# Eight layers on one core: output bias added tile by tile, residual joins reordered, token ids as one 16-bit value, expert weights held behind the second gather

## The reference, cut to what matters

```
x = x + cross_attention_0(norm(x));  x = x + quantised_ffn(norm(x))
x = x + (cross attention with bias, ffn)(norm(x))
x = x + L1_ffn(norm(x))      # LN, self-attention over 1024 keys, + o @ w_o + b_o; LN; top-2 of 8 experts, relu
x = x + L2_attention(norm(x)) # one head, 77 keys, integer mask
x = x + L2_ffn(norm(x))      # every expert whose sigmoid(x @ Wg + bg) > 0.5, relu
x = x + L3_attention(norm(x))
x = x + L3_ffn(norm(x))      # the best expert of 8, gelu
# an expert: y = func(x @ W1[e] + b1[e]) @ W2[e] + b2[e], weighted and added to its tokens
```

## Time and profile before

| | |
|---|---|
| median of 3 runs | 2282.51 us (2282.28 to 2283.62) |
| the profiled execution | 2278.04 us, its span 2276.3 us |
| PE busy | 1962.3 us, 86% |
| DVE, ACT, POOL busy | 47%, 40%, 33% |
| moved by DMA | 151.26 MB, mean 66 GB/s |
| m1, m2, m3 begin at | 984.8, 1375.2, 2076.0 us |

### The profile page before, as it was taken

The page is one execution under the profiler, slowest core; times in us unless marked ns, Lnnn a source line. Parts: engine busy times, 40 slices in busy tenths (PEclk is TensorE's granted clock), DMA queues, the critical chain, the costliest instruction groups (busy, mean ns, idle before and its releaser), DMA issues. The chain is left out here.

```text
span 2276.3 us, 39023 instructions
## 1 busy us (share of the span) xinstructions
PE 1962.3 (86%) x12253; PEld 1425.4 (63%) x12254; DVE 1069.3 (47%) x2424; ACT 910.1 (40%) x1930; POOL 755.3 (33%) x790
## 2 busy tenths in 40 slices
PE   6699989744999999849999945999999998696898
PEld 5476656512233232338999844999999997364797
DVE  6875834635777777253332246222222222576221
ACT  2413642132777777613333321333333333264132
POOL 0134952405000000043444333334444343585243
PEclk9799999876999999969999976999999999798899
DMA  4004300123111111075222118422122221205611
GB/s 159 19 1 146 101 1 1 32 76 94 37 36 49 42 37 36 2 245 156 33 35 36 28 53 292 115 36 36 31 36 35 35 34 27 68 1 177 221 32 26
DMA packets 124399, 151.26 MB, mean 66 GB/s; under 512 B 27066, under 2 KB 104731, under 8 KB 124171
## 3 DMA queue, kind: packets, MB, share of 16 engines
q1 hardware_dynamic: 93533, 117.61, 15.9%
q0 software_dynamic: 24288, 31.81, 8.6%
q10 hardware_dynamic: 6480, 0.59, 0.3%
HBM read 114.35 MB, written 37.36 MB: 67 GB/s over the span
## 5 line engine op out<-in xcount | busy, mean ns | idle before, releaser
L1902 PE MATMUL banks<-m_rowsT,x_normT 128*128 128x128 f32 x4032 | 479.0, 278 | 11.9 <-issue 7.6
L1902 PEld LDWEIGHTS banks<-m_rowsT,x_normT 128*128 128x128 f32 x4032 | 468.5, 194 | 29.0 <-issue 11.5
L1911 PE MATMUL banks<-m_w,m_hT 128*128 x2016 | 461.3, 382 | 7.3 <-ACT m_hT L2145 5.6
L1911 PEld LDWEIGHTS banks<-m_w,m_hT 128*128 128x128 f32 x2016 | 375.6, 191 | 56.4 <-issue 8.4
L2155 ACT ACTIVATE m_y<-banks,m_weight 128x256 f32<-128x256 f32 x126 | 59.6, 473 | 636.7 <-PE banks L1914 526.6
L2585 ACT ACTIVATE sh_pT<-banks 128x1024 f32<-128x1024 f32 x256 | 250.7, 1024 | 26.1 <-PE banks L2544 26.0
L2145 ACT ACTIVATE m_hT<-banks,m_bias 128x128 f32<-128x128 f32 x848 | 229.7, 387 | 65.6 <-PE banks L1902 61.4
L1821 POOL DMA_INDIRECT scratch_acc<-m_y,m_row_ids x106 | 169.6, 1600 | 124.8 <-ACT m_y L2155 82.9
L2609 DVE TENSOR_REDUCE sh_mhalf<-banks 128x1 f32<-128x512 f32 x308 | 194.2, 683 | 35.5 <-PE banks L2493 35.5
L2079 DVE TENSOR_SCALAR x_normT<-m_w 128x2048 f32 x129 | 158.3, 1227 | 77.0 <-issue 69.8
L1807 POOL COPY m_row_ids<-m_ids 128x1 int32 x117 | 52.1, 445 | 337.0 <-DMA scratch_acc<-m_y,m_row_ids 215.2
(11 more groups left out here) (404 smaller groups left out, 2745.1 us busy)
## 6 DMA issues: line engine op xcount, KB each, us to landing
m_w<-L_W SPq DMA_DIRECT2D x32, 1024.0 KB, 13.4
m_w<-L1f_W SPq DMA_DIRECT2D x16, 1024.0 KB, 13.6
a_bt<-bias SPq DMA_DIRECT2D x16, 616.0 KB, 3.9
scratch_parts<-sp_part SPq DMA_DIRECT2D x48, 128.0 KB, 1.9
sh_ks<-scratch_parts SPq DMA_DIRECT2D x96, 64.0 KB, 2.2
scratch_rows<-x_norm SPq DMA_DIRECT2D x12, 512.0 KB, 9.3
sh_qs<-scratch_parts SPq DMA_DIRECT2D x90, 64.0 KB, 2.3
scratch_acc<-x_resid SPq DMA_DIRECT2D x2, 2048.0 KB, 13.5
```

Of the source, the lines that this page charges most:

```text
L1902: mm = pe.matmul(ps[:, H_BANK[u] + f // 4, f % 4 * P:(f % 4 + 1) * P], w1_tile[:, u, k, f * P:(f + 1) * P], rowsT[:, u, k, :], start=(k == ...
L1911: mm = pe.matmul(ps[:, Y_BANK[u], 0:D], hT[:, u, f, :], w2_sb[:, bass.ds(e, 1), f, :], start=(f == 0), stop=(f == FB - 1 and not biased))
```

## The change

- The bias b_o is added to `xn` by 16 instructions, one tile each, each behind the `m_split` of one more pair of heads.
- `token_projection` adds x for 12 tiles, with `rstd` of the three groups after tiles 6, 10 and 11. The last four tiles are joined at the start of m1's POOL stream in one instruction, and DVE waits for it (`joined`) before it overwrites these tiles.
- `plain_cross_attention` makes no `rstd`; m2 makes all four groups itself (`ready=0` in place of 2).
- A token's id is one number in 16-bit floats of the other format (`F16`), 128 * tile + lane - 2048: one product instead of two per slot, a table half as wide on PE, and one instruction instead of two to read it.
- SP waits for `rows_in[1]` (the gather of slot 1 has landed) after the table's stores; only then follow expert 1, the store of x, and experts 2 to 7.

```diff
@@ routed_layer, SP
                     for g in range(NCH):
                         sp.wait_ge(tile_normed, 4 * g + 4)
                         sp.dma_start(table[g * CH:(g + 1) * CH, 0:D].rearrange("(t p) d -> p t d", p=P), xn[:, 4 * g:4 * g + 4]).then_inc(stored, 16)
+                    sp.wait_ge(rows_in[1], 16)
+                if e == 1:
                     sp.dma_start(stream.rearrange("(t p) d -> p t d", p=P), x[:]).then_inc(x_stored, 16)
@@ routed_layer, POOL
+            if joins_last:
+                pool.tensor_tensor(x[:, NT - 4:NT], x[:, NT - 4:NT], xn[:, NT - 4:NT], ALU.add).then_inc(joined, 1)
             for g in range(ready, NCH):
@@ routed_layer, PE
-                    at = ps[:, TABLE_BANK, g * 2 * W:(g + 1) * 2 * W] if local else ps[:, TABLE_BANK, 0:2 * W]
-                    mm = pe.matmul(at, lane_hits[:, g % 2, :, t], id_parts[:, g, :, :, t],
+                    at = ps[:, TABLE_BANK, g * W:(g + 1) * W] if local else ps[:, TABLE_BANK, 0:W]
+                    mm = pe.matmul(at, lane_hits[:, g % 2, :, t], tokens_at[:, g, :, t],
@@ routed_layer, DVE
             for t in range(NT):
+                if joins_last and t == NT - 4:
+                    dve.wait_ge(joined, 1)
...
-            link(dve.tensor_tensor(id_parts[:, :, 0], tile_hits, back_b[:].unsqueeze(1).unsqueeze(1).broadcast_to([P, G, W, NT]), ALU.mult))
-            dve.tensor_scalar(id_parts[:, :, 1], tile_hits, lane[:], None, ALU.mult).then_inc(parts_done, 1)
+            dve.tensor_tensor(tokens_at, tile_hits, tokens[:].unsqueeze(1).unsqueeze(1).broadcast_to([P, G, W, NT]), ALU.mult).then_inc(parts_done, 1)
...
-            link(dve.tensor_scalar(high_at, high, float(P), float(TOK), ALU.mult, ALU.add))
-            dve.tensor_tensor(ids_at, high_at, low, ALU.add).then_inc(ids_done, 1)
+            dve.tensor_scalar(ids[:, 0:COLS], ps[:, TABLE_BANK, 0:COLS], float(TOK), None, ALU.add).then_inc(ids_done, 1)
@@ self_attention, POOL
-                pool.tensor_tensor(acc[:], acc[:], w["bo"][:].unsqueeze(1).broadcast_to([P, NT, D]), ALU.add).then_inc(bias_added, 1)
+                for t in range(NT):
+                    pool.wait_ge(m_split, t + 1)
+                    pool.tensor_tensor(acc[:, t, :], acc[:, t, :], w["bo"][:], ALU.add).then_inc(bias_added, 1)
@@ program
-            routed_layer(core, "m2", "threshold", x, ..., ready=2)
+            routed_layer(core, "m2", "threshold", x, ..., ready=0)
```

More of the change, by code:

```diff
@@ L255, in __init__ @@
         self.rank, self.lane, self.counting = (self.loads[n] for n in ("rank", "lane", "counting"))
[L256 to L258 removed]
+        self.ones, self.before, self.lanes = sb("ones", [P, P], BF16), sb("before_b", [P, P], BF16), sb("lanes", [P, P], F16)
+        self.tiles, self.marked_tiles = sb("tiles", [P, 2 * NT + EXPERTS], F16), sb("marked_tiles", [P, NT], F16)
+        self.tokens, self.earlier = sb("tokens", [P, NT], F16), sb("earlier", [P, EXPERTS, EXPERTS])
         self.pick, self.pad_id, self.unit = sb("pick", [65, P], BF16), sb("pad_id", [P, 1]), sb("unit", [P, 1])
@@ L287, in make @@
         pool.tensor_scalar(self.marked_tiles[:], self.counting[:, 0:NT], -float(EXPERTS * NT), None, ALU.add).then_inc(made, 1)
-        pool.tensor_scalar(self.back[:], self.counting[:, 0:NT], -float(NT), None, ALU.add).then_inc(made, 1)
+        pool.tensor_scalar(self.firsts[:], self.counting[:, 0:NT], float(P), -float(TOK), ALU.mult, ALU.add).then_inc(made, 1)
+        pool.wait_ge(made, 13)
+        pool.tensor_scalar(self.tokens[:], self.firsts[:], self.lane[:], None, ALU.add).then_inc(made, 1)
     def order_experts(self, dve, made):
@@ L1263, in plain_cross_attention @@
         shares = sb("shares", [P, 4, D])
-        stats, moments, rstd, half = core.stats, core.moments, core.rstd, core.half
+        stats, moments = core.stats, core.moments
         params.place_passing(ctx)
-        b2_split, share_sb, joined, stats_done, moments_done, eps_done, rstd_done = (
-            sem(x) for x in ("b2_split", "share", "joined", "stats", "moments", "eps", "rstd"))
+        b2_split, share_sb, joined, stats_done, moments_done = (sem(x) for x in ("b2_split", "share", "joined", "stats", "moments"))
         s_mm, chain, s_ready, exp_done, rs_done, pT_mm, pT_sb, y_mm, y_sb = (
@@ L1280, in _ @@
             params.split_output_bias(pool, b2_split)
[L1282 to L1287, removed]
             for g in range(NCH):
@@ L1663, in routed_layer @@
         wg_sb, bg_sb, wide_gate = params["wg"], params["bg"], sb("wide_gate", [P, KD, 32])
[L1664 removed]
+        rank, counting, earlier = route.rank, route.counting, route.earlier
         if affine:
@@ L2718, in _, with reciprocals @@
         def _(pool):
-            for g in range(NCH):
+            def reciprocals(g):
                 own = slice(4 * g, 4 * g + 4)
-                if g < NCH - 1:
-                    pool.wait_ge(moments_done, 4 * g + 4)
-                    pool.tensor_scalar(rstd[:, own], moments[:, own, 1], EPS, None, ALU.add).then_inc(eps_done, 1)
-                    pool.wait_ge(eps_done, g + 1)
-                    pool.tensor_tensor(rstd[:, own], rstd[:, own], half[:].broadcast_to([P, 4]), ALU.pow).then_inc(rstd_done, 1)
-                for t in range(4 * g, 4 * g + 4):
-                    pool.wait_ge(y_sb, t + 1)
-                    pool.tensor_tensor(core.x[:, t, :], core.x[:, t, :], acc[:, t, :], ALU.add).then_inc(joined, 1)
+                pool.wait_ge(moments_done, 4 * g + 4)
+                pool.tensor_scalar(rstd[:, own], moments[:, own, 1], EPS, None, ALU.add).then_inc(eps_done, 1)
+                pool.wait_ge(eps_done, g + 1)
+                pool.tensor_tensor(rstd[:, own], rstd[:, own], half[:].broadcast_to([P, 4]), ALU.pow).then_inc(rstd_done, 1)
+            for t in range(NT - 4):
+                pool.wait_ge(y_sb, t + 1)
+                pool.tensor_tensor(core.x[:, t, :], core.x[:, t, :], acc[:, t, :], ALU.add).then_inc(joined, 1)
+                if t in (6, 10):
+                    reciprocals(t // 4 - 1)
+            reciprocals(2)
 def program(nc, dram):
```

33 lines of the change are left out of this document (13 added, 20 removed).

## The result

The changed kernel takes 2314.59 us (median of 4 runs, 2314.18 to 2316.72); the kernel before, run beside it, 2282.40 (4 runs, 2278.84 to 2283.62). The ratio is 1.0146, 95% interval 1.0128 to 1.0163: 32 us slower, where 41 were forecast. The profiled execution after has a span of 2314.9 us.

The account below looks back on a forecast made before the run. PE was taken as busy for most of the span, so gains come only where it stands still. Terms -7.8 - 5.9 - 0.7 + 37.8 + 17.9 = +41.3 us on a 2282.5 us median gave 2324 us, range 2301 to 2335.

Parts of the forecast that it names:

- The hold: Routed layers: SP's wait for slot 1's gather makes PE's first W1 product later, +37.8 us over m1, m2 and m3.
- T: Landing of slot 1's gather in each routed layer, forecast at 1020.0 in m1, 1414.1 in m2, 2103.7 us in m3.
- first product: PE's first product with W1 in each routed layer, claimed 18.2 us after slot 1's gather lands: +11.7, +14.9, +11.2 us.
- The fast rival: SP not held by bytes under way, eight issues of 0.4 to 0.5 us each: 2275 us, chance 0.08.
- The load moved into the slots: Slot 4 of each routed layer: its gather meets the shifted 16 MB load and PE stalls 7.4 us; +17.9 us over all.
- The bias: Self-attention: bias added tile by tile, so DVE's L2619 falls from 7.94 to 0.18 us; -7.8 us.
- no idle of PE ahead of L2502: Self-attention: sign that PE no longer waits there once L2619's longest is near 0.18 us.
- The joins: End of the projection: twelve joins fit beside it and the stage ends with DVE; -5.9 us.
- L2's attention and m2: No rstd between the attention's joins, -2.7 us; m2 makes four groups, +2.3 of which +2.0 taken; together -0.7 us.
- I count 0: Start of m1: four tiles joined there cost POOL 2.7 us, claimed covered by DVE's and PE's work; 0 us.
- The ids: Routed layers: narrower id table brings ids or first gather earlier by 3.1 us in m1, 0.8 in m2, 3.8 in m3.
- The sum: Whole kernel: all terms together +41.3 us, added to the median of 2282.5 us: 2324 us, slower by 1.8%.

## Why the prediction was right

**The direction and the step that decides it.** The hold moved the first step of `experts_ready` and the store of x behind T, with 8 MB ahead of the step. Forecast: first product at +11.7, +14.9 and +11.2 us; measured +11.7, +14.8 and +9.1. In m3 T came 0.4 us sooner than I had it, the step 14.3 us after T in place of 15.2, and the product 2.2 us after the step in place of 3.0. The fast rival (SP isn't held by bytes) is excluded by issues of 7.57 and 7.29 us and, as an experiment, by the 5.5 to 6.1 us per layer that 2 MB are worth.

**The load moved into the slots.** Forecast 17.9 us over the three layers. In the run with the hold alone the stages grew by 52.1 us and the first products came 12.0, 13.8 and 10.1 later, which leaves 16.1. The stall was 5.7 to 6.5 us there in place of 7.4; against the kernel before it grew by 13.9 us over the three layers. The low clock behind it, which my sum did not have, adds 3.0 (W2's products took 4.89, 4.97 and 5.32 us there, and 3.72, 3.72 and 4.76 at the same places before). So the total is partly luck: a stall that I had too long and a clock that I had left out nearly cancel. In the changed kernel the same subtraction leaves 19.3.

**The bias.** Forecast -7.8; alone it measured -8.3 in the medians (interval -10.3 to -3.2) and -9.8 in the stage. The traces bear out the 7.8 itself: PE's idle time fell from 8.59 to 0.82 us. My sign "no idle of PE ahead of L2502" was too strict. The further 2 us of the stage are not placed.

**The joins.** The end of the stage came nearly as forecast: -4.9 between the traces with the bias alone and the changed kernel (-5.9). So did L2's attention and m2: from POOL's first join to the start of m2 it took 12.4 us and now 9.6 (forecast -2.7), and DVE's last normalised tile in m2 comes 1.7 us later after its start (forecast +2.3, of which I took 2.0). The step that failed is "I count 0" for the four tiles in m1. I had judged by the mean pace of L1969 that it isn't locked out. By the Trainium skill's "SBUF — State Buffer", section "Who interferes with whom", a `tensor_scalar` can be, for the whole of a GpSimd instruction. The trace agrees with the page: 2454 ns in place of 401. The price was 2.0 us of DVE, and without the hold 3.5 of m1's first product (the joins alone), as the store of the gate weights starts 2.0 us later into a full queue and lands 4.2 later. With the hold the queue is empty and that part falls away; the 2.0 us of DVE do not, and there the earlier ids pay for them. Semaphores and barriers are thus not the only places where DVE and POOL meet.

**The ids.** Forecast -3.1, -0.8 and -3.8. The first two came in DVE's time (m1's 32 products take 2.75 us, L2047 is gone). Alone they measured nothing: in m1 and m3 the first gather waits for the store of the gate weights. I had written that of m3 and not asked it of m1, where the earlier trace rows don't show the wait ahead of the first gather. In the changed kernel they do count. SP's queue is empty, that store lands 3.0 us after its issue in m1 (13.6 before), and POOL's wait ahead of the first gather ends with the ids (7.49 us of it in the rows of m1 above, and the same releaser in m2 and m3). In m1 their 3.1 us are set against the 2.0 of the join's lock, so that T came only 0.4 us sooner than with the hold alone. In m3 the -3.8 came true (first gather at 23.0 in place of 26.8), but 3.3 of it come with the hold alone, which keeps SP's queue empty.

**The size.** The sum was +41.3, the stages of the two traces show +40.2, and the medians +32. The parts measured alone give +50.5 - 8.3 - 5.3 - 0.2 = +36.7 by medians; from t0 on their traces show +51.3, -5.6, -5.9 and +2.9, together +42.7. So the parts add up in the traces, and what the medians lack is 4 to 9 us. Of the 9, the two profiled executions account for 6.5 by their distance from their medians, 4.4 under and 2.1 over. What the hold costs within the changed kernel shows how such a gap comes about: 42.7 by medians and 42.0 between the two profiled executions, but 48.8 from t0 on, because the one without the hold came 6.9 us later to t0. Whether the medians hide the same thing can't be told from one trace of each kernel, and it stays open.

## What to carry to other kernels

Before a queue is held back, list what stands behind the wait and who needs it first: here a flag and a store that everyone waited for, not the weights that it was about. Gates that open at nearly the same time must be moved together; moving the flag alone gave back 4 us of 43, the store alone 15 (by 2 MB fewer ahead of the step), both with expert 1 all of it. A load that has to be moved anyway is only shifted by a hold: look at which small transfer meets it next. And a long two-input instruction on POOL beside DVE's work costs DVE up to its whole length; cut into tiles, it holds DVE for one tile at a time, and nothing where DVE has no such instruction just then.

## What the runs showed of the hardware

SP's DMA issues are short (0.37 to 0.58 us) for the first 4 MB after an empty queue (w1, w2 and x), and the next takes 7.1 to 8.2 us. In the run with x ahead of the hold four weights of 1 MB were short (0.37 to 1.42) and the fifth took 4.8 to 5.6. From there each MB takes 2.8 to 2.9 us.

Under such a load (340 GB/s from 1458 to 1465) slot 4's rows reached PE 5.8 to 6.0 us after POOL's gather began. With an empty queue slot 0's came 3.2 us after (999.77 to 1002.97).

DVE's `TENSOR_SCALAR` of 256 elements took 400 ns, over twice the time per element of L2070's 1228 ns for 2048. All the same it was locked out by POOL for 2.05 us. A slow pace is no proof against the lock. What PE lost by the lock in self-attention was 7.0 to 8.6 us in four traces for one instruction of 8.8 us on POOL.
